# Products of zeros where TensorE waits, and sparse fetches in turn with scatters

## The reference, cut to what matters

```python
x = _layernorm(x + _L0_attn_ref(x, ...))   # 16 heads, rotary tables, ALiBi
x = _layernorm(x + _L0_ffn_ref(x, ...))    # gated MLP
x = _layernorm(x + _L1_attn_ref(x, ...))   # selective scan
x = _layernorm(x + _L1_ffn_ref(x, ...))    # MoE, 8 experts, top 2 with a capacity
x = _layernorm(x + _L2_attn_ref(x, ...))   # attention whose softmax runs over the queries
x = _layernorm(x + _L2_ffn_ref(x, ...))    # sparse experts: 32 with a capacity, 16 adapters
x = _layernorm(x + _L3_attn_ref(x, ...))   # 16 heads, rotary tables
x = _layernorm(x + _L3_ffn_ref(x, ...))    # experts choose tokens
```

## Time and profile before

| | us |
|---|---|
| median of 3 runs | 1772.19 (1769.64 to 1773.47) |
| the profiled execution | 1780.89 |
| its span, first to last instruction | 1779.1 |
| TensorE busy | 1513.0 (85%) |
| VectorE busy | 1033.6 (58%) |
| ScalarE busy | 930.6 (52%) |
| GpSimd busy | 396.5 (22%) |

### The profile page before, as it was taken

The page is one execution under the profiler, slowest core; times in us unless marked ns, Lnnn a source line. Parts: engine busy times, 40 slices in busy tenths (PEclk is TensorE's granted clock), DMA queues, the critical chain, the costliest instruction groups (busy, mean ns, idle before and its releaser), DMA issues. The chain is left out here.

```text
span 1779.1 us, 21362 instructions
## 1 busy us (share of the span) xinstructions
PE 1513.0 (85%) x7296; PEld 663.0 (37%) x7296; DVE 1033.6 (58%) x2172; ACT 930.6 (52%) x1574; POOL 396.5 (22%) x351
## 2 busy tenths in 40 slices
PE   4899999899989897788899750694799988999998
PEld 1344444344333333243344320592122223444443
DVE  7576773111059999766677568143788854633332
ACT  6766666435668886420466720133377774433333
POOL 4111100000169898400122200431111200100000
PEclk7899999999989999999999975597699998999999
DMA  5211210200000000000211280403211203000000
GB/s 150 55 38 46 64 20 2 91 1 0 5 0 5 5 2 4 18 27 1 48 26 25 113 323 0 31 6 116 85 51 50 70 5 117 1 0 0 0 1 24
DMA packets 51490, 72.30 MB, mean 41 GB/s; under 512 B 11050, under 2 KB 44096, under 8 KB 49622
## 3 DMA queue, kind: packets, MB, share of 16 engines
q1 hardware_dynamic: 50102, 69.21, 12.8%
q0 software_dynamic: 1280, 1.73, 1.2%
HBM read 48.30 MB, written 18.12 MB: 37 GB/s over the span
## 5 line engine op out<-in xcount | busy, mean ns | idle before, releaser
L655 ACT ACTIVATE a_probs_sb<-a_t_ps 128x512 f32<-128x512 f32 x512 | 286.5, 595 | 126.0 <-PE a_t_ps L536 73.0
L746 DVE CUSTOM_DVE_ANT_0 a_biased<-a_s_ps,a_bias 128x512 f32<-128x512 f32 x256 | 166.4, 686 | 67.5 <-issue 67.4
L532 PE MATMUL a_t_ps<-a_stack 126*128 126x512 bf16 (+1 forms) x512 | 167.0, 388 | 26.4 <-ACT a_probs_sb L655 9.4
L513 PE MATMUL a_s_ps<-a_stack 96*128 96x512 bf16 (+1 forms) x512 | 154.5, 410 | 35.7 <-DMA a_stack<-a_stacks 24.8
L753 DVE TENSOR_REDUCE a_least_sb<-a_s_ps 128x2 f32<-128x1024 f32 x128 | 152.6, 1220 | 31.5 <-PE a_s_ps L513 31.2
L1544 POOL TENSOR_TENSOR s_dbu<-s_du,s_bs 128x1024 f32<-128x1024 f32 x64 | 152.5, 2392 | 33.6 <-DVE s_h L1624 27.2
L2997 ACT ACTIVATE c_hid<-c_up_ps,c_b 128x512 f32<-128x512 f32 x128 | 87.7, 687 | 128.6 <-PE c_up_ps L2914 125.4
L1624 DVE TENSOR_TENSOR_SCAN s_h<-s_ps,s_dbu 128x1024 f32<-128x1024 f32 x64 | 146.6, 2290 | 13.0 <-ACT s_ps L1407 8.9
L3128 DVE TENSOR_TENSOR c_hid<-c_hid,c_g_ps 128x2048 f32<-128x2048 f32 x32 | 73.1, 2286 | 126.9 <-PE c_g_ps L2932 126.9
L551 PE MATMUL a_o_ps<-a_probs_sb,a_vpad 128*16 128x512 f32 x1024 | 137.3, 609 | 0.2 <-ACT a_probs_sb L655 0.2
L1157 PE MATMUL s_ps<-s_hc,ident 128*128 128x512 f32 x256 | 121.2, 595 | 1.3 <-DVE s_hc L1633 1.3
(11 more groups left out here) (467 smaller groups left out, 2523.7 us busy)
## 6 DMA issues: line engine op xcount, KB each, us to landing
x_wu<-in_x_wu SPq DMA_DIRECT2D x2, 4096.0 KB, 18.1
a_stacks<-a_p SPq DMA_DIRECT2D x16, 384.0 KB, 2.9
a_stack<-a_stacks SPq DMA_DIRECT2D x32, 192.0 KB
a_stack<-a_stacks SPq DMA_DIRECT2D x64, 96.0 KB, 2.3
a_stacks<-a_p SPq DMA_DIRECT2D x16, 256.0 KB, 2.3
q_q<-q_q SPq DMA_DIRECT2D x32, 128.0 KB, 2.3
x_wd<-in_x_wd SPq DMA_DIRECT2D x2, 2048.0 KB, 33.5
a_rope<-in_a_rope SPq DMA_DIRECT2D x2, 1024.0 KB, 5.7
```

The lines of the kernel that those rows point to most:

```text
L513: made = nc.tensor.matmul(s_ps[:, 2 * (x % 2) + e, :], operand(0, k, pair, e, SCORE_ROWS)[:, t * P:(t + 1) * P], operand(1, k, pair, e, SC ...
L532: last = nc.tensor.matmul(out, operand(1, k, pair, e, TURNED_ROWS)[:, t * P:(t + 1) * P], operand(0, k, pair, e, TURNED_ROWS), start=True, ...
L655: nc.scalar.activation(probs[:, y % PROB_RING, e, :], bank("turned", y, e), ACT.Exp, scale=-1.0).then_inc(probs_ready, 1)
L746: nc.vector.tensor_tensor_reduce(out=biased[:, e, :], in0=s_ps[:, 2 * (x % 2) + e, :], in1=bias[:, h, at:at + N], scale=1.0, scalar=3.0e38 ...
```

## The change

A tile `nothing` of 128 x 128 zeros is set up at the start. `keep_busy` multiplies these zeros with a tile of ones into a PSUM region whose content is not needed at that point, so no result changes. It is called

- in every norm but the last: two products of 512 columns behind the last variance product;
- in the attentions: seven (first) or six (last) products of 512 columns behind the products of batch 0, one of 256 columns in each step below LAG that has nothing between, and in the first attention four of 512 at step LAG. The wait for the cleared sums moves ahead of them;
- in the MoE: three ahead of the last turn; in query softmax: one behind step 0 and two behind step 2 of the first batch;
- in the selection: 35, one for every second instruction of VectorE, for which TensorE waits on a semaphore of its own, `selected`; all chained instructions of the selection (written `select` in place of `then`) count it up;
- two behind the placement of the tiles, three ahead of the first turn of the experts, nine behind the last `back`.

The other part is the order on GpSimd: eight fetches, and then each scatter followed by one more fetch.

```diff
--- before.py
+++ after.py
@@ -78,7 +78,14 @@
         engine.wait_ge(semaphore, value)
 
 
-def layernorm_stage(core, xT, tag, out=None, prefetch=None, wide_range=False):
+def keep_busy(core, pe, out, times):
+
+    rows, size = out.shape
+    for _ in range(times):
+        core.nc.tensor.matmul(out, core.nothing[:, 0:rows], core.ones_row[:, 0:size], start=True, stop=True)
+
+
+def layernorm_stage(core, xT, tag, out=None, prefetch=None, wide_range=False, busy=True):
 
 
     out = xT if out is None else out
@@ -116,6 +123,9 @@
                 if i > 0:
                     variance(i - 1)
             variance(B - 1)
+            if busy:
+                pe.wait_ge(logvar_ready, done + 1)
+                keep_busy(core, pe, var[:, 0:N], 2)
 
         @block.scalar
         def _(act):
@@ -543,7 +553,6 @@
                 wait(pe, probs_ready, 4 * z + 4)
                 if t == 0:
                     wait(pe, values_kept, k)
-                    wait(pe, sums_cleared, 1)
                     if g == 0:
                         wait(pe, v_kept, i + 1)
                 for h in range(GROUP):
@@ -592,10 +601,14 @@
                 nc.tensor.matmul(products_bank(0, n), wqkv[:, n, :], xT[:, cols(0)],
                                  start=True, stop=True).then_inc(products_ps, 1)
             project_values(0)
+            wait(pe, sums_cleared, 1)
+            keep_busy(core, pe, o_ps[:, :], 7 if alibi else 6)
             for x in range(TOTAL):
                 i, s = divmod(x, BATCH_STEPS)
                 y = x - LAG
                 z = y - SUM_LAG
+                if x == LAG and alibi:
+                    keep_busy(core, pe, o_ps[:, :], 4)
                 if x < ATT_STEPS:
                     score(x, 0)
                     if not alibi:
@@ -610,6 +623,8 @@
                     sum_values(z // 2)
                 if s in between(i):
                     make_between(i, s)
+                elif x < LAG:
+                    keep_busy(core, pe, o_ps[:, 0:N // 2], 1)
 
         @block.scalar
         def _(act):
@@ -1756,6 +1771,8 @@
                     products(n + 1)
                 if n % NT == 0 and n // NT + 1 < B:
                     inside(n // NT + 1)
+                if n == TT - 1:
+                    keep_busy(core, pe, hid_ps[0][:, :], 3)
                 if n < TT:
                     turn(n)
 
@@ -2000,6 +2017,8 @@
             wait(pe, loaded, 48)
             for s in range(Q_SLOTS):
                 prepare(0, s)
+                if s in (0, 2):
+                    keep_busy(core, pe, s_ps[:, Q_BANKS - 1, :], 1 if s == 0 else 2)
             for g in range(Q_GROUPS):
                 scores(g)
                 if g % Q_PAIRS == 1 and g > 2 * Q_PAIRS:
@@ -2204,6 +2223,7 @@
     nc = core.nc
     E, CAP, CH = X_EXPERTS, X_CAP, X_CHUNKS
     CT = TT // B
+    SELECT_STEPS = 7 * (CAP // 8)
     r1x, r1s, r1b, pick, r2 = weights
     pick_x, pick_small = pick[:, 0:MEANS], pick[:, MEANS:2 * MEANS]
     pick_length, pick_spread = pick[:, 2 * MEANS:PICKS - 1], pick[:, PICKS - 1:PICKS]
@@ -2234,6 +2254,7 @@
     shift_cleared = core.flag("x_shift_cleared")
     shift_ready = core.flag("x_shift_ready")
     slots_ready = core.flag("x_slots_ready")
+    selected = core.flag("x_selected")
     tiles_ready = core.flag("x_tiles_ready")
     step = core.flag("x_step")
     with ExitStack() as mem:
@@ -2355,6 +2376,9 @@
             for j in range(TT // CH):
                 last = nc.tensor.transpose(turn_ps[:, j * P:(j + 1) * P], quarters[:, j, :], core.ident[:, :])
             last.then_inc(score_turned, 1)
+            for n in range(0, SELECT_STEPS, 2):
+                pe.wait_ge(selected, n + 1)
+                keep_busy(core, pe, sums_ps[0][:, :], 1)
             pe.wait_ge(lists_ready, 1)
             nc.tensor.transpose(lists_ps[0:CAP, 0:E], lists[:, :], core.ident[0:E, 0:E]).then_inc(lists_turned, 1)
             pe.wait_ge(shift_ready, 1)
@@ -2366,6 +2390,7 @@
                     last = nc.tensor.matmul(tiles_ps[:, :, tile], shift[:, P - at:2 * P - at], slots[:, c::PERIOD],
                                             start=((c, at) == parts[0]), stop=((c, at) == parts[-1]))
             last.then_inc(tiles_ready, 1)
+            keep_busy(core, pe, sums_ps[0][:, :], 2)
 
         @block.scalar
         def _(act):
@@ -2472,39 +2497,48 @@
             dve.wait_ge(place_loaded, 16)
             nc.vector.tensor_copy(xt[:, :, X_PLACE], place[:, :]).then_inc(payload_ready, 1)
 
+            routed, done[0] = done[0], 0
+
+            def select(instruction):
+
+                instruction.then_inc(selected, 1)
+                done[0] += 1
+                dve.wait_ge(selected, done[0])
+
             dve.wait_ge(score_turned, 1)
-            then(nc.vector.tensor_copy(work[:, :], turn_ps[:, :]))
+            select(nc.vector.tensor_copy(work[:, :], turn_ps[:, :]))
...
             dve.wait_ge(lists_turned, 1)
             nc.vector.tensor_copy(slots[:, :], lists_ps[0:CAP, 0:E]).then_inc(slots_ready, 1)
             dve.wait_ge(tiles_ready, 1)
             in_tiles = h_ps[0][:, 0:X_TILES]
+            done[0] = routed
             then(nc.vector.tensor_scalar(fetchf[:, :], in_tiles, -1.0, 0.0, ALU.add, ALU.max))
             nc.vector.tensor_copy(fetch_at[:, :], fetchf[:, :])
             nc.vector.tensor_scalar(gone[:, :], in_tiles, 0.5, X_GONE, ALU.is_lt, ALU.mult)
@@ -2597,10 +2631,12 @@
 
             pool.wait_ge(rows_stored, 16)
             pool.wait_ge(results_zeroed, 32)
-            for r in range(TILES):
+            for r in range(AHEAD):
                 fetch(r)
             for r in range(TILES):
                 scatter(r)
+                if r + AHEAD < TILES:
+                    fetch(r + AHEAD)
 
         @block.tensor
         def _(pe):
@@ -2647,6 +2683,7 @@
                     nc.tensor.transpose(back_ps[:, k * P:(k + 1) * P], yT[:, r * P:(r + 1) * P],
                                         core.ident[:, :]).then_inc(back_ready, 1)
 
+            keep_busy(core, pe, up_ps[2][:, :], 3)
             turn(0)
             pe.wait_ge(w_loaded, 16 * 8)
             for n in range(UNITS):
@@ -2661,6 +2698,7 @@
                     down(n - 1)
             down(UNITS - 1)
             back(G - 1)
+            keep_busy(core, pe, up_ps[2][:, :], 9)
             for i in range(B):
                 pe.wait_ge(mixed, i + 1)
                 for t in range(CT):
@@ -3348,6 +3386,7 @@
         core.one = core.sb(ctx, "one", [P, 1])
         core.centre = core.sb(ctx, "centre", [P, P])
         core.ones_row = core.sb(ctx, "ones_row", [P, N])
+        core.nothing = core.sb(ctx, "nothing", [P, P])
         core.x_loaded = core.flag("x_loaded")
         core.more_x_loaded = core.flag("more_x_loaded")
 
@@ -3367,6 +3406,7 @@
                 nc.gpsimd.memset(core.eps[:, :], LN_EPS)
                 nc.gpsimd.memset(core.one[:, :], 1.0)
                 nc.gpsimd.memset(core.ones_row[:, :], 1.0)
+                nc.gpsimd.memset(core.nothing[:, :], 0.0)
                 nc.gpsimd.memset(core.centre[:, :], -1.0 / C).then_inc(zeroed, 1)
                 nc.gpsimd.memset(core.ident[:, :], 0.0).then_inc(zeroed, 1)
                 pool.wait_ge(zeroed, 2)
@@ -3375,7 +3415,7 @@
                 nc.gpsimd.affine_select(out=core.ident[:, :], in_=core.ident[:, :], compare_op=ALU.not_equal,
                                         fill=1.0, base=0, pattern=[[-1, P]], channel_multiplier=1)
         ctx.enter_context(core.run_stages(STAGES, A, xT))
-        layernorm_stage(core, xT, "last_ln")
+        layernorm_stage(core, xT, "last_ln", busy=False)
         stored = core.flag("out_stored")
         with core.block() as block:
             @block.sync
```

26 lines of the change are left out of this document (13 added, 13 removed).

## The result

The changed kernel took 1759.78 us in the median of four runs (1756.73 to 1768.24) against 1772.39 (1769.64 to 1773.47): ratio 0.994, 95% interval 0.9911 to 0.9969. Two later measurements on two chips, with eleven and twelve runs, gave 0.9967 (0.9932 to 1.0002) and 0.9966 (0.9941 to 0.9991). It is faster, by 6 to 12 us and not by 28; of the three intervals one just reaches 1. A few later executions stood far above the others of their kernel (2300 us, for instance), and no ratio counts them. Its profiled execution took 1768.24 us, span 1766.4, clock 0.958.

A forecast was written before the change was run, and what follows sets the result against it. The expert stage was taken as bound by TensorE, its first four groups at half clock with an idle hole. Terms summed to -32.8 us on the profiled execution (1748.1); the median forecast was 1744 us, range 1732 to 1760.

The forecast's parts named there:

- Experts at the full clock: Expert groups 0 to 3: without the hole, 27.8 us at half clock become 15.5 at full clock, -12.3 us.
- rival 1: Clock falls in the placement and experts start cold: most of the 12.3 us lost, 1759 us; chance 0.14.
- Fetches in turn with scatters: Expert groups: TensorE's 9.41 us idle hole, read as the price of piled-up fetches, goes with the new order: -9.4 us.
- rival 4: Experts: VectorE's weighing waits for its fetched tile, some 2 us in each of three periods, 1750 us; chance 0.06.
- Placement: Placement of tiles ahead of the experts: 24 small products gain 1.3 us, two fillers behind them cost 1.2.
- Last attention: Last attention: fillers cost 0.14 us in each of ten steps, denser work raises the clock earlier; -1.5 us net.
- Tail and norm: Behind the experts: nine fillers in the wait for results speed the norm (-1.8) and last output turn (-0.5).
- norms and logits: Norm fillers may hold the clock over the logits behind them in MoE and choice: -1 us for both.
- query softmax: Query softmax: fillers inside TensorE's waits warm the mean and variance products and the projections, -4.2 us together.
- first attention: First attention: warm, the fillers fit TensorE's idle time; cold, they are 5.9 us too long; taken as -2 us.
- the selection at no cost for the lists: Selection: 35 fillers, one for every two VectorE steps, raise the clock and catch up before the lists: cost 0.
- rival 3: All fillers: products of zeros neither raise nor hold the clock, so the kernel is slower, 1797 us; chance 0.03.

The follow-up runs named there:

- plain loads: Kernel before, its 20 indirect fetches replaced by SP loads of 128 consecutive rows: ratio 0.9897; the same loads in the changed kernel with all its fillers: 0.9917.
- the order alone: Kernel before with only the new GpSimd order (eight fetches, then each further one in turn with a scatter), no fillers: ratios 1.0002 and 0.9986.
- the pace: Kernel before with all 20 fetches ahead of the scatters, at most two fetches in flight, no fillers: ratio 0.9999.

## Why the prediction was wrong

The sign and the kind of gain were right; the gain forecast, 28 us in the median, was more than double the measured 12.6. The sum missed the profile by 20.2 us. The step that failed is the one on the experts, both of its terms.

- **Experts at the full clock, -12.3.** Measured in the profile: -11.4 - (-9.4) = -2.0. I took the whole because the load holds the clock once it is there, and bet on five fillers to carry it across. They did not, in two places. The clock fell in the placement (1104.0), 2.6 us behind a wait of 2.15 us for the lists, and in all 13 profiles with the selection's fillers it was at 0.50 for 6.8 us there. The fillers ahead of the turn raised it again, but TensorE then waited 1.09 and 1.13 us for the first two tiles, and the clock fell right behind. So rival 1, with 0.14, came true, at the placement and once more at the turns. That its 1759 is the measured time is in part luck: it counts half of the 8.7 us for the hole and nothing for what the last attention lost. The argument for the other end, that the same load did not raise the clock, was half right: how long it takes is not fixed. With nearly the same work it was 23.9, 3.4 and 17.1 us in three profiles of the changed kernel, and 4.1 with plain loads. Why is open.
- **Fetches in turn with scatters, -9.4.** The profile had it, the time did not: the order alone measured 1.0002 and 0.9986, and the pace, which removes the hole without bringing stops, 0.9999 on its chip. I split the doubt (1739.4 and 1748.8) and took the middle; the upper one is nearer. Besides, the new order brought stops of its own in six of ten profiles, two waits of 1.7 to 2.7 us on TensorE with 3.4 to 17.1 us of low clock behind each. All six are from two chips, three of the four without are from a third, and the chip of the first measurement is not on record. The Trainium skill ("Runtime: NRT & Kernel Launch", "Instruction fetch mechanics") has sequencers bring in code by DMA, and the trace of the kernel without step fillers has two such loads of 8 KB at 1143.40 and 1143.82, just ahead of a stop at 1144.15; but the first profile of the changed kernel has such a pair too (1150.73 and 1151.11), beside its own 13th fetch, with no stop. And the traces have no such load in the hole of before (one at 1114.50, the next at 1155.48) nor in the second stop of the changed kernel's second profile (none between 1164 and 1170.5). So loads of code, which the prediction offered for the hole, do not explain it. The forecast had only the weighing as a new wait; in the profiles looked at VectorE did not wait there, so rival 4 was out.
- **Placement.** -1.8 for the 24 products, between the bounds; but its two fillers ran cold, 3.76 us for the 1.7 assumed, and the barrier came later by the difference: +1.2 in all instead of -0.1.
- **Last attention, -1.5.** Measured +3.7 in this profile. The step's sum set VectorE's 1.15 us against a cold pair and a cold filler, 0.43 + 0.86 = 1.29. Its 0.86 was half of the 1.71 of a filler of 512 columns; one of 256 took 1.15 at the low clock, and the pair 0.53, together 1.68. So the filler's cost was mis-sized, by 0.29 us. The six fillers ended 6.96 us ahead of the stacks, as said. But the same stretch differs between profiles by some 4 us for kernels without fillers too (253.1 to 257.2), so of the 3.7 only the 1.5 of the run without step fillers is tied to them, by one profile. With the step fillers it was 254.4 to 258.2 in ten profiles, with 14 fillers in the wait in their place 252.8 to 254.3 in four.
- **Tail and norm, -2.3; norms and logits, -1.** Nothing. The nine fillers ended in time, but TensorE waited 1.91 us for the results, then turned them in short pieces, and the clock fell at 1199.6 in the middle of it.
- **Right:** query softmax (-3.7 for -4.2; from the mean product to the first scores it took 15.0 to 15.1 us in all 15 profiles with these fillers, 18.3 to 18.8 in the five without), first attention (-1.6 for -2 in this profile, though over all profiles with its fillers it ended from 2.2 us earlier to 0.5 later than before), the selection at no cost for the lists, zeros that raise the clock (rival 3 is out), and the norms' fillers inside their waits. By the rule of the Trainium skill ("TensorE: Matmul & The Clock Gate", Part 1) that the gate goes by how busy the engine is, zeros count; the same 17.1 us with zeros and with 1/128 agree. The 1.5 us ahead of the routing are not the change's: kernels with and without fillers showed either value.

From the runs: the fillers are worth 0.9940 against 0.9999 with the paced order on one chip, 0.0059 x 1770 = 10 us (about 5 either way), most of it from the selection's (7), then query (3.7). The order in the changed kernel is worth about nothing in the time. What remains of the first measurement, 12.6 us against 6 later, is within the intervals.

## What to carry to other kernels

Size a gain by what every execution pays, not by a hole of one profile: a wait that no row explains can be in the typical execution on one chip and not on another, and one profile does not tell which. Comparing executions at the same mean clock gives an estimate without a further profile. In the expert groups a raised clock was lost behind gaps of 1 us or more, though not behind every such gap in the kernel (query softmax starts warm behind a wait of 1.05 us), so each wait on the way into a heavy stage has to be looked at; bridging the first of them alone moved the fall and gave no gain that the runs can tell. A filler in a paced loop must be priced from a row of its own size at the low clock: here half of a larger one's price was 0.29 us too little. Try the pace of the indirect transfers and a plain substitute before work on the clock. The plain loads bring other rows, so they are a test and no replacement, but on their chip they alone gave more than the whole change.

## What the runs showed of the hardware

- TensorE's news of finished products can arrive 3.5 us late, and 10.9 us in the hole of before, while GpSimd issues indirect transfers. It came in long form with 20 fetches in a row (a hole of 9.4 and of 10.4 us in the two profiles), in short form where fetches and scatters took turns (groups 6 and 10, at the same two instructions of ScalarE in all six profiles that had it, 4.0 to 4.1 us each, the first 0.7 to 0.8 us behind the start of the 13th fetch's issue; in two of them also in group 1, 3.1 and 3.2 us), once with paced fetches (3.0 us), and not in the two profiles with plain loads. The paced order was profiled on two chips; on one of them the turns of fetch and scatter showed no stop either, on the other they were not profiled, so that it avoids the stops is not shown. The cause stays open.
- The granted clock of a TensorE that is busy all the time stayed at 0.50 for 3.4, 10.2, 17.1, 23.9 or 27.3 us in expert groups, and for 23.9, 3.4 and 17.1 us in three executions of the same kernel.
- In the groups each fall of the clock that was looked at followed a gap of TensorE of 1 us or more; without such a gap it held for 75.1 us with TensorE busy 71.35 of them. The fall itself can come later, while TensorE is busy: in the placement it came 2.6 us behind the gap.
- Products of zeros raised the clock in the selection after the same 17.1 us as products of 1/128.
